# An eight-group attention layer with a ternary feed-forward: value products batched six times per half pass, four banks for the first tiles, 16-bit feed-forward operands

## What is computed

```python
y = x * rsqrt(mean(x*x) + eps) * rms_w
q, k, v = split(y @ w_in.T)           # 8 groups: 4 query heads, one key and one value head of 64
q, k = rope(q), rope(k)
o = softmax(causal(q @ k.T / 8)) @ v
x = layernorm(x + (x + o @ w_out.T))
xq = ternary(x, 0.33, 0.5)            # +0.5, 0 or -0.5
w  = ternary(weight, 0.2, 0.6) + rram_variation
x  = layernorm(x + xq @ w.T)
```

## Time and profile before

| | us |
|---|---|
| median of 3 runs | 1302.51 (1302.15 to 1303.39) |
| the profiled execution, device time | 1301.82 |
| its span, first to last instruction | 1300.0 |
| TensorE busy | 1241.3 (95%) |
| VectorE busy | 1121.5 (86%) |
| ScalarE busy | 1025.4 (79%) |
| GpSimd busy | 760.3 (58%) |

### The profile page before, as it was taken

How to read it: one execution, slowest core, us unless ns; L and a number is a source line. 1 busy time by engine, 2 the same in 40 slices (tenths; PEclk the granted TensorE clock), 3 DMA queues, 4 the chain that set the end, 5 groups by cost and what they waited for, 6 DMA issues and landing times.

```text
span 1300.0 us, 29127 instructions
## 1 busy us (share of the span) xinstructions
PE 1241.3 (95%) x9632; PEld 808.7 (62%) x9632; DVE 1121.5 (86%) x2934; ACT 1025.4 (79%) x2199; POOL 760.3 (58%) x776
## 2 busy tenths in 40 slices
PE   4599999999999999999999999999999999999897
PEld 2356666666666666666666666666666666666575
DVE  3698988988898898989888888989888888888997
ACT  4687878887787878888787878887788877878765
POOL 1265656466645656367445756466554756698566
PEclk9799999999999999999999999999999999999999
DMA  6001111111010111101111110112001111211002
GB/s 218 29 17 63 47 41 34 50 47 45 31 54 30 58 34 35 48 31 62 34 45 35 54 42 31 46 33 66 28 28 50 46 46 42 63 38 54 18 26 110
DMA packets 46966, 62.06 MB, mean 48 GB/s; under 512 B 12256, under 2 KB 28896, under 8 KB 46816
## 3 DMA queue, kind: packets, MB, share of 16 engines
q1 hardware_dynamic: 46816, 60.20, 14.0%
HBM read 34.74 MB, written 4.46 MB: 30 GB/s over the span
## 4 chain that ended last, share of the span: by engine, by line
PE 75%; DVE 12%; POOL 4%; issue 4%; ACT 3%; DMA 1%; SPq 0%; DVEq 0%; POOLq 0%; ACTq 0%
PE x L1175 17%; PE t L1220 17%; PE s L1163 15%; PE ot L1128 13%; PE x L1203 10%; DVE prob_lo L1091 3%; DVE prob L998 3%; DVE win_lo L1018 2%; DVE acc L1083 1%; PE x L1112 1%; ACT prob L826 1%; PE x L1193 1%; PE x L1152 1%; POOL ffn_raw L680 1%; POOL ffn_raw L682 1%
## 5 line engine op out<-in xcount | busy, mean ns | idle before, releaser
L794 ACT ACTIVATE prob_hi<-t 128x512 f16<-128x512 f32 x576 | 337.3, 589 | 121.6 <-PE t L1220 117.9
L1091 DVE SCALAR_TENSOR_TENSOR prob_lo<-t,prob_hi 128x512 f16<-128x512 f32 x576 | 392.7, 685 | 31.1 <-ACT prob_hi L794 27.6
L826 ACT ACTIVATE prob<-prob,neg_max 128x896 f32<-128x896 f32 (+7 forms) x512 | 392.4, 768 | 31.7 <-DVE neg_max L998 30.2
L998 DVE CUSTOM_DVE_ANT_0 prob<-s,mask,neg_kappa 128x512 f32<-128x512 f32 (+3 forms) x512 | 322.4, 643 | 54.0 <-PE s L1163 36.6
L1163 PE MATMUL s<-k_t,q_t 128*128 128x512 f16 (+3 forms) x1536 | 341.6, 328 | 21.5 <-DVE neg_max L998 10.7
L1220 PE MATMUL t<-ident,prob 128*128 128x128 f32 x2304 | 355.0, 278 | 4.2 <-ACT prob L826 2.0
L1220 PEld LDWEIGHTS t<-ident,prob 128*128 128x128 f32 x2304 | 264.0, 141 | 93.5 <-issue 35.4
L767 POOL TENSOR_TENSOR o_lo<-o_raw,o_hi 128x256 f16<-128x256 f32 x128 | 86.3, 675 | 226.0 <-ACT o_hi L894 224.3
L1163 PEld LDWEIGHTS s<-k_t,q_t 128*128 128x128 f16 x1536 | 142.3, 99 | 100.4 <-DVE neg_max L998 18.4
L1128 PE MATMUL ot<-prob_hi,v_sb 128*64 128x256 f16 x2304 | 203.0, 276 | 0.0
L998 DVE CUSTOM_DVE_ANT_0 prob<-s,mask,low_max 128x128 f32<-128x128 f32 (+3 forms) x256 | 153.4, 606 | 15.5 <-PE s L1163 12.6
(11 more groups left out here) (103 smaller groups left out, 1631.4 us busy)
## 6 DMA issues: line engine op xcount, KB each, us to landing
swapped<-flat SPq DMA_DIRECT2D x128, 128.0 KB, 2.1
spread<-recip_rows SPq DMA_DIRECT2D x256, 64.0 KB, 2.6
recip_rows<-turned SPq DMA_DIRECT2D x512, 0.5 KB
raw<-L_attn_w_in SPq DMA_DIRECT2D x8, 768.0 KB, 4.6
swapped<-flat SPq DMA_DIRECT2D x64, 64.0 KB, 2.0
raw<-L_attn_w_out SPq DMA_DIRECT2D x8, 512.0 KB, 3.5
out<-acc SPq DMA_DIRECT2D x16, 256.0 KB, 2.0
acc<-L_attn_x SPq DMA_DIRECT2D x3, 1024.0 KB, 10.1
```

The lines of the kernel that those rows point to most:

```text
L794: act.activation(prob_hi[:, u % P_RING, :], t_ps[u % 2][:, :], ACT.Copy, scale=P_SCALE).then_inc(prob_hi_done, 1)
L826: act.activation(row, row, ACT.Exp, bias=neg_max[:, kk % 4, h:h + 1], scale=-1.0, accum_out=total[:, kk % 4, h:h + 1]).then_inc(ex_done, 1)
L998: dve.tensor_tensor_reduce(out=prob_row(s, h)[:, c * BANK:c * BANK + cols], in0=s_ps[:, off:off + cols], in1=mask[:, seen:seen + cols], sc ...
L1091: dve.scalar_tensor_tensor(out=prob_lo[:, u % P_RING, :], in0=t_ps[u % 2][:, :], scalar=P_SCALE, in1=prob_hi[:, u % P_RING, :], op0=ALU.mu ...
```

## The change

1. **Batches.** `BATCHES` has six sizes for each half pass and not eleven, and `P_RING` is 12 and not 8.
2. **First tiles.** Tiles 0 to 3 are transposed into four banks (`t_ps`, `ot_ps`) by a new event `early`, without waiting for one another; sixty matmuls of 256 columns without use (`WARM`) stand first on TensorE; `consts` comes later in `FIRST`; the projections wait for one quarter of the weights at a time; key and value chunk and its swapped copy have tiles of their own, so that ScalarE's copy doesn't wait for other chunks; the rope of one query chunk moves from VectorE to GpSimd.
3. **Feed-forward.** `ffn_hi`, `ffn_lo`, `xq` and the ternary tiles are 16-bit floats (weights scaled by 2^4, given back in the residual); the ternary tiles are turned by plain 16-bit matmuls with a 16-bit identity.
4. **Order.** All three tables are new.

```diff
-P_RING = 8
-BATCHES = (1, 2, 3, 4, 5, 3, 3, 4, 3, 4, 4)
+P_RING = 12
+BATCHES = (3, 7, 5, 6, 7, 8)
+EARLY = 4
+WARM = 60
 FIRST = (
-    ('consts',), ('sw', 2, 0, 2), ('xn', 0), ('sq', 0), ('nq',), ('xn', 1), ('xn', 2), ('norm', 0), ('nw',),
-    ('norm', 1), ('w', 0), ('norm', 2), ('xn', 3), ('w', 1), ('w', 2), ('norm', 3), ('w', 3), ('sq', 1),
-    ('pj', 2, 0, 2), ('xn', 4), ('pj', 2, 0, 0), ('xn', 5), ('ro', 2, 0, 2), ('sw', 2, 0, 0), ('norm', 4),
+    ('sq', 0), ('xn', 0), ('early', 0), ('xn', 1), ('nq',), ('sw', 2, 0, 2), ('xn', 2), ('nw',), ('sw', 2, 0, 0),
+    ('xn', 3), ('consts',), ('early', 1), ('early', 2), ('sw', 2, 0, 1), ('early', 3), ('w', 0), ('w', 1), ('w', 2),
+    ('w', 3), ('xn', 4), ('sq', 1), ('pj', 2, 0, 2), ('xn', 5), ('xn', 6), ('ro', 2, 0, 2), ('ro', 2, 0, 0),
+    ('pj', 2, 0, 0), ('pj', 2, 0, 1), ('hl', 2, 0, 2), ('norm', 4), ('norm', 5), ('hl', 2, 0, 0), ('norm', 6),
...
 OPENING = dict(
-    SQUARES=(5, 9),
-    NORMS=((0, 11), (13, 19), (23, 23), (24, 26), (30, 40), (49, 61), (91, 143), (161, 174)),
+    SQUARES=(0, 9),
+    NORMS=((14, 14), (15, 16), (18, 26), (31, 33), (35, 50), (55, 71), (80, 132), (145, 148)),
...
 FINAL = dict(
-    LAYER=((323, 346, 371, 379, 392, 396, 417), (342, 356, 386, 394, 406, 408, 498),
+    LAYER=((306, 335, 356, 380, 386, 391, 472), (320, 336, 376, 389, 403, 436, 496),
...
-        ffn_hi = sb("ffn_hi", [P, KC, D], F32R)
-        ffn_lo = sb("ffn_lo", [P, KC, D], F32R)
+        ffn_hi = sb("ffn_hi", [P, KC, D], F16)
+        ffn_lo = sb("ffn_lo", [P, KC, D], F16)
-        xq = sb("xq", [P, 2, KC, P], F32R)
+        xq = sb("xq", [P, 2, KC, P], F16)
...
+                        elif e[0] == "ro" and plan is first:
+                            pool.tensor_tensor(turned_x, turned_x, sin_sb[:, q_half(0)], ALU.mult
+                            pool.tensor_tensor(x, x, cos_sb[:, q_half(0)], ALU.mult).then_inc(late_products, 1)
+                            pool.tensor_tensor(x, x, turned_x, ALU.add).then_inc(roped, 1)
...
-            pe.wait_ge(ident_in, 16)
+            pe.wait_ge(ones_set, 1)
+            warm = ones[:, :].bitcast(F16)
+            for _ in range(WARM):
+                pe.matmul(t_ps[1][:, 0:2 * P], warm[:, 0:P], warm[:, :], start=True, stop=True)
...
-                    mm = pe.transpose(bank[:, c * P:(c + 1) * P], tern_tile(t)[:, c * P:(c + 1) * P], ident[:, :])
+                    mm = pe.matmul(bank[:, c * P:(c + 1) * P], tern_tile(t)[:, c * P:(c + 1) * P], ident16[:, :],
+                                   start=True, stop=True)
...
+                        elif e[0] == "early":
+                            t = e[1]
+                            if t == 0:
+                                pe.wait_ge(ident_in, 16)
+                            pe.wait_ge(xn_done, t + 1)
+                            for k in range(KC):
+                                mm = pe.transpose(early_bank(t)[:, k * P:(k + 1) * P], xn_tile(t)[:, k * P:(k + 1) * P],
+                                                  ident[:, :])
+                            mm.then_inc(early_full, 1)
```

More of the change, by code:

```diff
@@ L29 @@
 Q_SCALE = 2.0 ** 10
+F_SCALE = 2.0 ** 4
 FLAT_SCALE = Q_SCALE / (Y_SCALE * W_SCALE)
@@ L510, in tern_tile, with early_bank, flat_tile, swapped_tile @@
         def tern_tile(t):
-            return raw[:, t % 3, :]
+            return raw[:, t % 3, 0:D // 2].bitcast(F16)
         def xn_tile(t):
-            return scratch(9 + t % 3) if t < FIRST_TILES else raw[:, 2, :]
+            return scratch(8 + t % 4) if t < FIRST_TILES else raw[:, 2, :]
+        def early_bank(t):
+            return (t_ps + ot_ps)[t]
+        def flat_tile(plan, n):
+            return scratch(6) if plan is first and n % 3 == 2 else flat[:, n % 2, :]
+        def swapped_tile(plan, n):
+            return scratch(14) if plan is first and n % 3 == 2 else swapped[:, n % 2, :]
         def prob_row(s, h):
@@ L594, in one @@
                             rows = P if e[3] < 2 else DH
+                            if plan is first and n % 3 == 2:
+                                sp.wait_ge(swapped_in[0], 32)
                             for i in range(2):
-                                sp.dma_start(swapped[i:rows:2, n % 2, :], flat[1 - i:rows:2, n % 2, :]
+                                sp.dma_start(swapped_tile(plan, n)[i:rows:2, :], flat_tile(plan, n)[1 - i:rows:2, :]
                                              ).then_inc(swapped_in[n % 2], 16)
@@ L670, in one @@
                         if (e[0] not in ("ln", "res", "sq", "ro", "hl", "oh", "fl", "x1", "nw", "no")
-                                or plan is first and e[0] in ("ro", "hl")):
+                                or plan is first and e[0] in ("ro", "hl") and e != ("ro", 2, 0, 1)):
                             continue
@@ L728, in one @@
                                                ).then_inc(rstd_done, 1)
+                        elif e[0] == "ro" and plan is first:
+                            n = chunk(2, 0, 1)
+                            x, turned_x = flat_tile(plan, n), swapped_tile(plan, n)
+                            pool.wait_ge(table_in[0], 32)
+                            wait(pool, flat_done, g, CHUNKS, n + 1)
+                            wait(pool, swapped_in[n % 2], g, swaps(10), swaps(n))
+                            pool.tensor_tensor(turned_x, turned_x, sin_sb[:, q_half(0)], ALU.mult
+                                               ).then_inc(late_products, 1)
+                            pool.tensor_tensor(x, x, cos_sb[:, q_half(0)], ALU.mult).then_inc(late_products, 1)
+                            pool.wait_ge(late_products, 2)
+                            wait(pool, roped, g, CHUNKS, n)
+                            pool.tensor_tensor(x, x, turned_x, ALU.add).then_inc(roped, 1)
                         elif e[0] == "ro":
@@ L744, in one @@
                             n = chunk(b, half, c)
-                            x, at = flat[:, n % 2, :], q_half(half)
+                            x, at = flat_tile(plan, n), q_half(half)
                             wait(pool, parts_hi, g, CHUNKS, n + 1)
@@ L866, in one @@
                             bank = wait_x_full(act, plan, g, e)
-                            wait(act, parts_done, g, CHUNKS, n - 1)
-                            if n % 3 == 2:
-                                wait(act, v_hi_done, g, 4, 2 * b + half + 1)
-                            act.activation(flat[:, n % 2, :], bank[:, :], ACT.Copy, scale=FLAT_SCALE
+                            if plan is not first:
+                                wait(act, parts_done, g, CHUNKS, n - 1)
+                                if n % 3 == 2:
+                                    wait(act, v_hi_done, g, 4, 2 * b + half + 1)
+                            act.activation(flat_tile(plan, n), bank[:, :], ACT.Copy, scale=FLAT_SCALE
                                            ).then_inc(flat_done, 1)
@@ L918, in residual @@
             def residual(t, bank):
-                dve.scalar_tensor_tensor(out=acc[:, t, :], in0=bank[:, :], scalar=SC_X, in1=acc[:, t, :],
+                dve.scalar_tensor_tensor(out=acc[:, t, :], in0=bank[:, :], scalar=SC_X / F_SCALE, in1=acc[:, t, :],
                                          op0=ALU.mult, op1=ALU.add).then_inc(x2_done, 1)
@@ L939, in events @@
                             dve.tensor_copy(mask[:, KEYS - P:KEYS], scratch(13)[:, 0:P]).then_inc(consts_cast, 1)
-                            dve.wait_ge(consts_cast, 1)
-                            dve.wait_ge(rms_in, 16)
-                        elif e[0] == "ro" and plan is first:
+                            dve.wait_ge(ident_in, 16)
+                            dve.tensor_copy(ident16[:, :], ident[:, :]).then_inc(ident_cast, 1)
+                        elif e[0] == "ro" and plan is first and e[3] != 1:
                             _, b, half, c = e
@@ L986, in events @@
                             kk, n = b * NT + s, scored(b, s, h, c)
+                            if plan is first:
+                                dve.wait_ge(consts_cast, 1)
                             cols, off = min(BANK, (s + 1) * P - c * BANK), n % 2 * BANK
@@ L1167, in events @@
                             _, b, half, c = e
-                            wait(pe, win_done, g, 4, 8 if b == 2 else 4)
+                            if plan is not first:
+                                wait(pe, win_done, g, 4, 8 if b == 2 else 4)
                             start = (b % 2) * NT + half * HALF
@@ L1173, in events @@
                             for k in range(KC):
+                                if plan is first:
+                                    wait(pe, win_done, g, 4, 4 + k + 1)
                                 for n, (w, y) in enumerate(((win_hi, yt_hi), (win_hi, yt_lo), (win_lo, yt_hi))):
```

85 lines of the change are left out of this document (50 added, 35 removed), and 98 rows, old and new, of tables (FIRST, LAYER, PROJECT, SCORES).

## The result

The changed kernel takes 1304.68 us (median of 14 runs, 1301.39 to 1307.46) against 1302.91 for the kernel before, run beside it (14 runs, 1300.15 to 1304.65): a ratio of 1.0017, interval 1.0010 to 1.0024. I had forecast 1272. The profiled execution took 1306.89 us, its span is 1304.2 (2.7 us lie around it, and not 1.8 as before).

A forecast was written before the change was run, and what follows sets the result against it. TensorE was taken to bound the six middle passes, VectorE the final pass from 1200 to 1275, chains the beginning and last 25 us. Savings of 5 + 6.5 + 15 + 4 = 30.5 us gave 1272 (1265 to 1279, chance 0.50).

The forecast's parts named there:

- The price of a batch: TensorE going into and out of value products: 0.25 us lost per batch whatever its size; 80 fewer batches save 20 us.
- So I take 0 us for new waits: Middle passes: VectorE's work in stock just covers its lag in longer batches, so TensorE gets no new waits, 0 us.
- the bound of +2.5: Middle passes: upper bound on new waits, 2.5 us a pass, the whole batch gain given back.
- the stock of 2.85 us: VectorE's work available during a batch: two t banks at 0.685 us and two score halves at 0.741, x banks besides.
- the lag: How far VectorE must be behind when a batch begins: about 2.0 us for six units, 2.6 for eight.
- Rival (1): VectorE and ScalarE starve in long batches, TensorE waits; half the batch gain lost (9 us), final pass gives 1: 1284; chance 0.17.
- Rival (4): Slower: TensorE waits for a t bank's refill and emptyings after every batch; decides from 0.32 us each, 1310 at 0.4; chance 0.03.
- The new tables only order work: Order tables on every queue: no row prices them apart from the new waits' bounds, -1.5 to +2.5 us a pass.
- DMA and GpSimd covers: Moved swaps, spreads and weight loads cost nothing: DMA share 0.13, GpSimd idle 64 us a pass, unless a rope lands late.
- The beginning: Up to the first unit: earlier projections and one query rope on GpSimd win 5 us, bounds 1 to 9.
- The opening pass: First pass: moved squares and scaled rows win 4 us (bounds 0 to 7), ten fewer batches 2.5.
- The final pass: Last pass: 8 us less TensorE work, but VectorE is full in the feed-forward; 4 us won, bounds 0 and 9.

## Why the prediction was wrong

- **The price of a batch was right.** I had 0.25 us; the first three rows of the table of delays fell from 6.8 to 4.4 us together with ten batches fewer, 0.24 each.
- **"So I take 0 us for new waits" failed.** Measured: 3.1 us in the pass of the tables; 2.6 to 3.6 in five of the six middle passes and 5.2 in the one from 807.63. That is outside the bound of +2.5 (and over the 1 us that I had named as the first sign of being wrong), though TensorE's own idle time, which I gave as a mark, only went from 1.5 to 2.4. The step failed twice. First, the stock of 2.85 us was counted from banks (two t banks, two score halves), as if each were ready for VectorE when a batch begins. In the row above it had 1.6 us, since a t bank is no work for VectorE until ScalarE has written the high part, and the score blocks there were smaller. Second, the lag was that of an average mixture of work, 89% of it VectorE's, and it took for granted that VectorE uses the time of a batch. In the stretches from each batch's first product to 0.6 us behind the start of its last, VectorE's idle time adds up to 2.3 us a pass before and to 4.9 after.
- **Rival (1)** named this mechanism, VectorE and ScalarE starving in long batches (the prediction calls it the second rival once, where it weighs the rule), and the page rule weighed beside it bore on it too: the Trainium skill (TensorEngine Tiling, PSUM Bottleneck) says that emptying PSUM may become the bound. The trace agrees only by part: relieving VectorE by 0.27 us a unit wins 1.9 us in the changed pass and 0.6 in the old one, so it accounts for 1.3 of the 3.1. The rival was priced at half the gain (9 us in seven passes); it took the gain and 0.7 us a pass more. Rival (4), a refill after every batch, would have needed 0.32 us a batch; the new waits are 3.1/12 = 0.26 in a middle pass.
- **"The new tables only order work"** was the second failed step. I had no row that priced them and gave them the waits' bounds. The runs price them: 4.0 us a pass for the new order with the old batches, 7.4 for the old order with the new ones. The order isn't neutral, and the two edits can't be added up from their single effects.
- **DMA and GpSimd covers.** I had named a late rope as what would end them. GpSimd's wait for the swaps grew over the span from 25.1 to 82.0 us. The group of the page of the kernel before, that of the changed one, and one place there where it reached TensorE:

```profile
L737 POOL TENSOR_TENSOR swapped<-swapped,sin_sb 128x512 f32<-128x512 f32 (+1 forms) x93 | 118.7, 1277 | 26.9 <-DMA swapped<-flat 25.1
```
```profile
L768 POOL TENSOR_TENSOR swapped<-swapped,sin_sb 128x512 f32<-128x512 f32 (+1 forms) x93 | 118.7, 1277 | 83.2 <-DMA swapped<-flat 82.0
```
```profile
846.89 1.29 POOL L768 TENSOR_TENSOR swapped<-swapped,sin_sb 128x512 f32<-128x512 f32 x1 [2.60 <-DMA swapped<-flat]
...
850.70 0.67 POOL L798 TENSOR_TENSOR o_lo<-o_raw,o_hi 128x256 f16<-128x256 f32 x1
...
851.52 0.38 PE L1264 MATMUL x<-wout_hi,o_hi 128*128 128x512 f16 x1 [1.69 <-POOL o_lo L798]
```

  In the pass from 807.63 the swap came 2.6 us late, the low part of the output stood behind the rope in GpSimd's queue, and the output projection waited 1.69 us for it. It came by another way than the wait of a score for q_t that I had named. In the pass from 658 the same swap was awaited for 0.28 us and cost nothing; the pass from 807 took 151.5 us and not 149.5, so 2 of the 6.1 us of the middle passes are this. The swap was issued within 0.5 us of its usual place in the pass, but landed 4.27 us after its issue and not 2.10. One pass each of two other runs of the new order has the same at the same place: without the sixty matmuls (4.21 us, a pass of 151.6) and with VectorE relieved (4.31 us, 149.9 among passes of 147.7 to 148.4). Five swaps of the kernel before take 3.6 to 4.0 us too, and its middle passes still differ by 0.6 us at most. Why one such transfer takes twice as long is open.
- **The beginning** was right down to the rope (projections from 18.4 against 18.1, the rope at 26.8 against 26.4), then the first score came into VectorE at 40.25 and not at 38. 1.8 us of that is in two operations of VectorE, next section. The first unit came at 44.68 and not 41.5: 1.8 us won of 5. In the executions that ran at full clock it was 40.75 to 42.81.
- **The opening pass** was about right: 164.3 against 162, the wait for the scales gone, but only 4.1 of 6.5 us won. Moving the squares by itself loses 11; the whole table wins.
- **The final pass.** I took 4 us for the feed-forward, the batches and the earlier layer together, with bounds 0 and 9; measured -0.6 for the feed-forward by itself and +4.0 for all of it. The work that I counted did leave TensorE (69.35 to 66.97 between 1200 and 1275). VectorE has as much idle time before 1200 (12.0 us against 10.2), which I had meant to be filled, is as full in the middle, and the last stretch is 29.2 us and not 25.0. But the layer isn't all of it: in the first 36 of the 72 units, ahead of its first step, TensorE's delays, counted as in the table, already add up to 9.5 us and not to 8.0, with the saving of the batches in them. The cause isn't VectorE's amount of work alone. With VectorE relieved the new order's final pass is still 3.4 us longer (192.1 against 188.7), with ScalarE relieved as well it is the shorter one (187.1 against 188.8). So the loss hangs on ScalarE's high parts more than on VectorE, by one execution of each; which places make it is open.

## What to carry to other kernels

A switch of an engine that costs 0.25 us is worth saving only if what stands behind it in the other queues is placed anew, and then both together have to be timed; a busy share of 89% is not a cover for stretches of 2 to 3 us in queues of fixed order. Before a long burst on one engine, count what is ready for each other engine, not what lies in the banks: a bank that a second engine must read first is no stock until that engine has come to it in its own queue. When the parts of a change are timed one by one, time the pairs that were made for each other together, and look for the stretches where each part holds by itself: here the beginning, the opening pass and the feed-forward gave 6 to 7 us that the rest had hidden.

## What the runs showed of the hardware

**Two operations of VectorE took more than twice as long beside GpSimd.** The query's parts take 0.69 us each in the kernel before, where GpSimd was idle. In the changed kernel, VectorE's and then GpSimd's timeline:

```profile
34.06 1.55 DVE L999 TENSOR_TENSOR q_t<-flat,q_t 64x512 f16<-64x512 f32 x1
35.63 1.64 DVE L1001 TENSOR_TENSOR q_t<-flat,q_t 64x512 f16<-64x512 f32 x1
...
38.82 0.69 DVE L999 TENSOR_TENSOR q_t<-prob,q_t 64x512 f16<-64x512 f32 x1
```
```profile
33.80 1.26 POOL L756 TENSOR_TENSOR prob<-prob,cos_sb 128x512 f32<-128x512 f32 x1
35.14 1.59 POOL L759 TENSOR_TENSOR prob<-prob 128x512 f32<-128x512 f32 x1
```

Each ends 0.54 to 0.55 us after the operation of GpSimd that was under way when it began: 35.61 behind 35.06, 37.27 behind 36.73. All eight executions with the new beginning show 1.55 and 1.64. Together that is 1.8 us more on the chain to the first score, and it is the cost of giving that rope to GpSimd which I had left out. The Trainium skill (SBUF — State Buffer, Who interferes with whom) states that a VectorE instruction with two SBUF inputs and a GpSimd instruction that reads SBUF share a port pair, and that the later one stands until the first is done; the trace agrees.

**The clock at the first projections isn't the same in every execution.** With the sixty matmuls ahead, the profiled executions of four kernels have their first projections at full clock (0.38 us each, the first unit at 40.75, 42.35, 40.93 and 42.81; the second of them was back at half clock 1.4 us later) and of three at half clock (0.58 and more; 44.68, 44.35 and 43.41). Without them it was half clock (44.24). So what I took as nothing, their benefit, can be some 2 us; one execution of each kernel, and a single one without them, doesn't tell how often, nor that the sixty are the reason. The changed kernel's runs spread wider than those of the kernel before, 6.1 us over 14 runs against 4.5, but the sixty aren't the reason for that: without them it was 7.4 us over 10 runs.
